# State-space stage of a decoder: the causal mask as block-step rows, and the last steps of silu, gate and output on GpSimd

## The chip, the cores and the metric

One Trainium2 chip, of which the kernel uses one core. The metric is device time in microseconds from start to end of one execution; the figure for the kernel before is the median of three runs. The engines are named TensorE (PE), VectorE (DVE), ScalarE (ACT), GpSimd (POOL) and SyncE (SP, which only issues DMAs here).

## What is computed

A two-layer decoder on x of shape (4, 256, 256), float32. Six stages, A to F: attention, experts chosen by token, a mixture of experts, a state-space mixer, attention over given keys, another mixture of experts. The change lies in the state-space stage, D, whose reference is, cut to what matters:

```python
xBCzA = einsum('bld,ed->ble', input_, in_proj_w)          # 1536 + 512 + 64 columns
xBC = silu(causal_conv(xBC, conv1d_weight, KSIZE=4) + conv1d_bias)
x, Bm, Cm = split(xBC)                                    # 64 heads of 8; 8 groups of 64 states
dt = softplus(A_log)
A_cum = cumsum(-dt) in chunks of 128
Lm = exp(segsum(A))                                       # exp(A_cum[i] - A_cum[j]), 0 where j > i
Y_diag = einsum('bcshn,bczhn,bhcsz,bczhp->bcshp', Cm, Bm, Lm, X)
Y_off = einsum('bcshn,bchpn,bhcs->bcshp', Cm, states, exp(A_cum))
yf = Y_diag + Y_off + D * x / dt
out = einsum('bld,ed->ble', yf * silu(z + z_bias), out_proj_w)
```

## The kernel before

The program is one list of steps, written by `schedule`, and each engine walks the same list and issues the steps that it has a part in, with semaphore waits between them. So the order of work on each engine is that of the list. Every engine runs its own instructions strictly in this order.

Stage D works in eight **units** u (four sequences of two chunks of 128 tokens), each of 16 **slots**. A slot holds one group of four heads:

- `ssd` on TensorE: the exponent table E of 128 x 512 (four heads of 128 x 128) in a PSUM bank. Line 1482, the **mask product**, writes the causal mask (0 or -1e30) by an identity matrix; line 1484, the **row product**, adds A_cum[i] - A_cum[j] from 15 rows (`rows_z`, `rows_s`): A_cum in three bfloat16 parts for each side, and rows of ones.
- `exp` on ScalarE (line 1066): M = exp(E), from PSUM to one of 8 buffers, four of them in `s_arena` and four in `s_early`.
- `mul` on VectorE (line 1849), two slots later: M = M * CBs, where CBs holds the products of C and B for the unit.
- `scan` on TensorE (line 1136), five slots later (LAG): eight small matmuls on M.

Two PSUM banks alternate for E, so that TensorE can be at most two tables ahead of the exponentials.

Between these, `UNIT_SLOTS` puts the rest of a unit at fixed slots, most of it for the unit before or after: `cb`, `cbc` (the CB products and their copy, line 1839), `state`, `yo` (the state of the chunk before, odd units alone; line 1858), `at` (rows by DMA), `dz`, `zt`, `zth`, `zsm` (the gate: half of z, its tanh on ScalarE, and (tanh + 1) * half on VectorE, line 1801), `y_t`, `yfs` (the output: lines 1875, 1880 and 1881: y + Du, in odd units + yo, then times the gate), `dy_t` (transposes, line 1512), `dy`, `dx` (projection and residual) and `xt`, `xtp` (inputs of the next unit; `xtp` is GpSimd's: lines 843, 845, 852). `PAIR_SLOTS` puts the convolution of three **pairs** of channel tiles beside each of the first five units: `din`, `din2` on TensorE, `ev` on ScalarE (lines 996, 998), three taps on VectorE (line 1781), `th` (tanh on ScalarE, line 1009) and `silu` on VectorE (line 1791, (tanh + 1) * half). Of the 24 pairs, eight were done beside the stage before, where ScalarE computes the silu whole, one ahead of unit 0, and 15 beside units 0 to 4, the last silu of a unit falling in slot 2 of the next. `raw` has two buffers, so `ev` of a pair waits for the silu two pairs back (`xs_ready`).

After unit 7 the last scans, its output and its projection run alone (the drain), then stage E starts when its residual is added. Layer norms of stage E are in the list behind units 2, 4 and 6; their power is GpSimd's (line 739). The first splits of stage E's queries are in unit 7 (`FIRST_SPLITS`, lines 1596 to 1608 on VectorE, 766 and 768 on GpSimd).

## Time and profile before

| | |
|---|---|
| median of 3 runs | 995.91 us (994.95 to 996.75) |
| the profiled execution | 990.7 us, of which the profile's span is 988.9 us |
| mean granted TensorE clock | 0.899 |
| stage D, from the first row product to the last residual | 456.2 to 704.1 us |
| TensorE / VectorE / ScalarE / GpSimd busy, whole span | 82% / 58% / 39% / 22% |
| mask product, line 1482 | 128 instructions, 52.3 us busy in the page's group, 408 ns mean |
| row product, line 1484 | 128 instructions, 51.9 us, 406 ns |
| M product, line 1849 | 64 + 64 instructions, 683 ns median |
| exponential, line 1066 | 64 + 64 instructions, 597 and 601 ns mean |

The profile's times are of one execution, taken by the hardware profiler. A busy share is an average over stages with different limits, so a stretch is read by itself. Matmuls are pipelined: the duration of one is longer than what it takes of TensorE's time, which is read from start to start. The same holds in a smaller measure for VectorE. "idle before <-" names what released an engine after a wait.

### The profile page before, as it was taken

The numbers are of one execution on the slowest core, as the hardware profiler recorded it, in microseconds if no ns is written. First come the engines' busy times: TensorE is split into PE (matmuls) and PEld (weight loads), VectorE is DVE, ScalarE is ACT, GpSimd is POOL, SyncE is SP. The second block draws the span as 40 slices with busy tenths as digits, with TensorE's granted clock in tenths as the row PEclk, the third lists the DMA queues.
The fourth block names the chain that finished last, engine by engine and source line by source line (L and its number), as shares of the span: only waits on it lengthen the run. The fifth ranks groups of instructions, "written<-read, shape, count | busy, mean of one in ns | idle before, by whom it ended". The sixth has DMA issues, their size and how long they took to land.

```text
span 988.9 us, 14763 instructions
## 1 busy us (share of the span) xinstructions
PE 810.5 (82%) x5680; PEld 523.6 (53%) x5680; DVE 577.0 (58%) x1188; ACT 383.7 (39%) x653; POOL 216.6 (22%) x210
## 2 busy tenths in 40 slices
PE   1577777599799799656999999998667786899998
PEld 0334443258677588533445444444445454677776
DVE  5666642544545457525878788568566653545443
ACT  1124334101444355233566465354124344444442
POOL 3200000223433322141101111011411201442432
PEclk9889979799999899866989899699778788899999
DMA  9000001001121211000000000000000001222331
GB/s 311 29 2 1 3 1 49 1 0 32 49 81 53 71 54 33 9 0 5 5 3 6 4 5 6 3 5 4 1 2 2 1 1 50 81 80 64 84 96 40
DMA packets 17831, 32.77 MB, mean 33 GB/s; under 512 B 5819, under 2 KB 9787, under 8 KB 17494
## 3 DMA queue, kind: packets, MB, share of 16 engines
q1 hardware_dynamic: 17762, 31.83, 10.4%
q8 instruction: 46, 0.75, 0.3%
q14 instruction: 23, 0.19, 0.1%
HBM read 29.85 MB, written 1.05 MB: 31 GB/s over the span
## 4 chain that ended last, share of the span: by engine, by line
PE 60%; DVE 20%; issue 9%; ACT 4%; POOL 4%; DMA 1%; SPq 1%; DVEq 0%; ACTq 0%; POOLq 0%
PE bank L1374 13%; PE bank L1398 8%; PE bank L1136 4%; PE bank L1484 3%; PE bank L1321 3%; PE bank L1482 3%; PE bank L1411 3%; PE bank L1418 2%; DVE s_xn L1555 2%; PE bank L1336 2%; DVE s_arena L1627 2%; PE bank L1265 2%; POOL s_rstd L739 1%; PE bank L1208 1%; PE bank L1384 1%
## 5 line engine op out<-in xcount | busy, mean ns | idle before, releaser
L791 POOL TENSOR_TENSOR s_wl<-s_wmoe,s_wh 128x768 fp32r<-128x768 f32 x54 | 99.2, 1839 | 175.0 <-ACT s_wh L961 175.0
L910 ACT ACTIVATE s_arena<-bank 128x512 f32<-128x512 f32 x96 | 56.6, 597 | 106.2 <-PE bank L1241 55.2
L1746 DVE TENSOR_TENSOR s_act<-bank,s_sg_moe 128x512 f32<-128x512 f32 x54 | 37.3, 691 | 82.4 <-PE bank L1374 75.8
L1627 DVE TENSOR_REDUCE s_arena<-bank 128x2 f32<-128x512 f32 (+1 forms) x96 | 64.6, 686 | 35.6 <-PE bank L1212 18.9
L1374 PE MATMUL bank<-s_xh,s_wh 128*128 128x512 f32 x216 | 73.1, 421 | 8.2 <-POOL s_wl L791 8.2
L973 ACT CAST s_ah<-s_act 128x512 fp32r<-128x512 f32 x54 | 33.6, 621 | 101.7 <-DVE s_act L1751 79.2
L1374 PE MATMUL bank<-s_xl,s_wh 128*128 128x512 f32 x216 | 69.3, 403 | 0.0
L1398 PE MATMUL bank<-s_wh,s_ah 128*128 128x256 f32 x216 | 66.5, 308 | 2.8 <-DVE s_al L1757 2.8
L1374 PE MATMUL bank<-s_xh,s_wl 128*128 128x512 f32 x216 | 68.4, 399 | 0.0
L1781 DVE SCALAR_TENSOR_TENSOR s_arena<-s_arena,s_convw 128x256 f32<-128x256 f32 x144 | 63.7, 483 | 0.6
L1398 PE MATMUL bank<-s_wl,s_ah 128*128 128x256 f32 x216 | 61.6, 285 | 0.0
L1398 PE MATMUL bank<-s_wh,s_al 128*128 128x256 f32 x216 | 61.5, 285 | 0.0
L1757 DVE TENSOR_TENSOR s_al<-s_act,s_ah 128x512 fp32r<-128x512 f32 x54 | 37.3, 691 | 40.3 <-ACT s_ah L973 40.2
L1066 ACT ACTIVATE s_arena<-bank 128x512 f32<-128x512 f32 x64 | 38.2, 597 | 50.1 <-PE bank L1484 50.1
L1482 PE MATMUL bank<-s_maskt,s_identb 128*128 128x512 bf16 x128 | 52.3, 408 | 5.1 <-DMA s_arena<-s_arena 4.3
L739 POOL TENSOR_TENSOR s_rstd<-s_ve,s_mhalf 128x2 f32<-128x2 f32 x24 | 16.6, 691 | 175.0 <-DVE s_ve L1547 174.7
L1849 DVE TENSOR_TENSOR s_arena<-s_arena 128x512 f32<-128x512 f32 x64 | 42.9, 685 | 15.9 <-ACT s_arena L1066 15.6
L1484 PE MATMUL bank<-s_arena 15*128 15x512 bf16 x128 | 51.9, 406 | 0.0
L1066 ACT ACTIVATE s_early<-bank 128x512 f32<-128x512 f32 x64 | 38.4, 601 | 30.2 <-PE bank L1484 29.9
L1398 PEld LDWEIGHTS bank<-s_wh,s_ah 128*128 128x128 f32 x216 | 41.4, 192 | 13.5 <-issue 8.2
L1374 PEld LDWEIGHTS bank<-s_xl,s_wh 128*128 128x128 f32 x216 | 42.5, 197 | 9.8
L1168 PE MATMUL bank<-s_ident,s_xn 128*128 128x128 f32 x80 | 15.5, 327 | 39.0 <-DVE s_xn L1555 36.9
(232 smaller groups left out, 1745.6 us busy)
## 6 DMA issues: line engine op xcount, KB each, us to landing
s_wmoe<-in_wF SPq DMA_DIRECT2D x28, 384.0 KB, 3.1
s_wmoe<-in_wC SPq DMA_DIRECT2D x26, 384.0 KB, 3.0
s_win<-in_win SPq DMA_DIRECT2D x1, 2112.0 KB, 10.4
s_x<-in_x SPq DMA_DIRECT2D x4, 256.0 KB, 3.5
s_early<-in_ctxT SPq DMA_DIRECT2D x1, 1024.0 KB, 9.5
s_ctxn<-in_ctx SPq DMA_DIRECT2D x1, 1024.0 KB, 12.3
s_arena<-s_arena SPq DMA_DIRECT2D x64, 6.0 KB
out_x<-s_x SPq DMA_DIRECT2D x4, 256.0 KB, 2.8
```

What stands on the lines that cost most here:

```text
L791: g.tensor_tensor(wl[:, w % NS_, :], wmoe[:, w % NW, :], wh[:, w % NS_, :], ALU.subtract).then_inc(wl_ready, 1)
L910: a.activation(PT[:, p % NPT, :], AR[n % 3][:, :], ACT.Exp).then_inc(a_read, 1)
L1066: a.activation(M[k % NM], S[k % 2][:, :], ACT.Exp).then_inc(e_read, 1)
L1136: ins = mm(bk[j * 32:(j + 1) * 32, quarter * P:(quarter + 1) * P], xsp[u % 2][:, quarter, h, j, :, :].rearrange("p q w -> p (q w)"), M[k % ...
L1374: ins = mm(G[2 * (n % 2) + half][:, :], a_[:, k, half, :], b_[:, k, toks], start=(p_ == 0), stop=(p_ == len(parts) - 1))
L1398: ins = mm(Y[t // NT][:, (t % NT) * D:(t % NT + 1) * D], a_[:, w % NA, t * P:(t + 1) * P], b_[:, w % NS_, 2 * KD * P:], start=(j == 0 and ...
L1482: mm(bk[:, :], identb[:, :], maskt[:, :].unsqueeze(1).to_broadcast([P, HG, P]), start=True, stop=False, skip_group_check=True)
L1484: mm(bk[:, :], rows_z[:, hg, :], rows_s[:, :, hg, :], start=False, stop=True, skip_group_check=True).then_inc(e_full, 1)
L1627: v.tensor_reduce(nM[:, q, h0:h0 + heads], V[n % 2][:, :].rearrange("p (h k) -> p h k", h=heads), AX.X, ALU.max, negate=True).then_inc(v_r ...
L1746: v.tensor_tensor(act_[:, w % 2, :], G[2 * (n % 2) + 1][:, :], sg_moe[:, n % 2, :], ALU.mult).then_inc(g_read, 1)
L1781: ins = v.scalar_tensor_tensor(o, raw[:, m % NRAW, h, KS - 1 - k:KS - 1 - k + L], convw[:, ct, KS - 1 - k:KS - k], o, ALU.mult, ALU.add)
L1849: v.tensor_tensor(m, m, CBs[:, u % 2, hg // (NV // NG):NG:NG // HG, :], ALU.mult).then_inc(m_ready, 1)
```

## The change

Three things are changed in stage D.

The mask product is dropped. Instead the row product gets 15 more rows (`STEPS` = 16): for each step s the row in `rows_s` is -1e30 for all columns ahead of 8 s and 0 from there, and the row in `rows_z` ("blocks") is 1 in the eight columns of block s. Together they mask all blocks of eight that lie ahead, but not the triangle within a block. What is left there is cut by the copy of CBs, which becomes a product with -1 and the triangular table `tri`, and by the M product, which becomes min(M, 1) * CBs, so that no large exponential meets a zero.

The last step of silu (one fused VectorE instruction), of the gate (one) and of the output (one sum in odd units and one product in all) move to GpSimd. GpSimd has no fused form here: silu and gate become a product and a sum, two instructions each, with a wait between. The output's part is a new step, `yfp`. `yo` waits for it.

In `UNIT_SLOTS` the output's later steps move by a slot: `dy_t` 9 to 10, `yfc` 10 to 11, `dy` 12 to 13, `dy2` 13 to 14, `dx` 14 to 15. One more DMA brings the blocks, and the table of one-hot rows grows from 192 to 432 KB.

```diff
-              (12, "dy", -1), (13, "dy2", -1), (14, "xt", 1), (15, "xt1", 1),
+              (13, "dy", -1), (14, "dy2", -1), (14, "xt", 1), (15, "xt1", 1),
...
-RR = 3 + 3 * HG
+RL = 3 + 3 * HG
+STEPS = 16
+RR = RL + STEPS - 1
...
                     sp.dma_start(rows_z[0:3, :, :], A["ones3"]).then_inc(hot_in, 16)
+                    sp.dma_start(rows_z[RL:RR, :, :], A["blocks"]).then_inc(hot_in, 16)
...
+                elif kind == "silu":
+                    b, j = i
+                    m = b * (CT // 2) + j
+                    if m < beside_c:
+                        continue
+                    pool.wait_ge(tanh_ready, m - beside_c + 1)
+                    half, th = xs[:, b % 2, 2 * j:2 * j + 2, :], raw[:, m % NRAW, :, KS - 1:]
+                    link(g.tensor_tensor(th, th, half, ALU.mult))
+                    g.tensor_tensor(half, th, half, ALU.add).then_inc(xs_ready, 1)
+                elif kind == "zsm":
+                    pool.wait_ge(z_tanh, i + 1)
+                    link(g.tensor_tensor(zs[:, i % 2, :], zs[:, i % 2, :], zt[:, :], ALU.mult))
+                    g.tensor_tensor(zs[:, i % 2, :], zs[:, i % 2, :], zt[:, :], ALU.add).then_inc(zs_ready, 1)
+                elif kind == "yfp":
+                    pool.wait_ge(v_read, at["V"]["y_t", s, i] + 1)
+                    if i % 2:
+                        pool.wait_ge(v_read, at["V"]["state", s, i, 1] + 1)
+                        link(g.tensor_tensor(yf, yf, yo, ALU.add))
+                    pool.wait_ge(zs_ready, i + 1)
+                    g.tensor_tensor(yf, yf, zs[:, i % 2, :], ALU.mult).then_inc(yf_ready, 1)
...
-                    mm(bk[:, :], identb[:, :], maskt[:, :].unsqueeze(1).to_broadcast([P, HG, P]),
-                       start=True, stop=False, skip_group_check=True)
-                    mm(bk[:, :], rows_z[:, hg, :], rows_s[:, :, hg, :], start=False, stop=True,
-                       skip_group_check=True).then_inc(e_full, 1)
+                    mm(bk[:, :], rows_z[:, hg, :], rows_s[:, :, hg, :], start=True, stop=True
+                       ).then_inc(e_full, 1)
...
-                        v.tensor_copy(CBs[:, i % 2, par:NG:2, :], V[n % 2][:, :].rearrange("p (g s) -> p g s", g=NG // 2)
-                                      ).then_inc(v_read, 1)
+                        v.scalar_tensor_tensor(CBs[:, i % 2, par:NG:2, :],
+                                               V[n % 2][:, :].rearrange("p (g s) -> p g s", g=NG // 2), -1.0,
+                                               tri[:, 0, :].unsqueeze(1).to_broadcast([P, NG // 2, P]),
+                                               ALU.mult, ALU.mult).then_inc(v_read, 1)
...
-                    v.tensor_tensor(m, m, CBs[:, u % 2, hg // (NV // NG):NG:NG // HG, :], ALU.mult).then_inc(m_ready, 1)
+                    v.scalar_tensor_tensor(m, m, 1.0, CBs[:, u % 2, hg // (NV // NG):NG:NG // HG, :], ALU.min, ALU.mult
+                                           ).then_inc(m_ready, 1)
                 elif kind == "yo":
+                    if i >= 2:
+                        dve.wait_ge(yf_ready, i - 1)
...
-                    if c:
-                        dve.wait_ge(v_read, at["V"]["state", s, i, 1] + 1)
-                        link(v.tensor_tensor(yf, yf, yo, ALU.add))
-                    v.tensor_tensor(yf, yf, zs[:, c, :], ALU.mult).then_inc(yf_ready, 1)
```

## Rows read from the trace of the kernel before

**Rows 1.** The page, busy time by engine, share of the span, instructions.

```profile
PE 810.5 (82%) x5680; PEld 523.6 (53%) x5680; DVE 577.0 (58%) x1188; ACT 383.7 (39%) x653; POOL 216.6 (22%) x210
```

**Rows 2.** Windows, one for each unit 0 to 7 but 4, columns in the first line.

```profile
core 0: us, PE busy (x) PEld busy (x) DVE busy (x) ACT busy (x) POOL busy (x), PEclk, DMA share, GB/s
456.20:485.40 29.20, 28.11 (x188) 13.35 (x187) 19.13 (x37) 16.29 (x32) 0.72 (x3) 0.85 0.02 4
485.40:519.70 34.30, 32.53 (x248) 16.27 (x247) 25.53 (x55) 17.88 (x35) 3.89 (x7) 0.90 0.02 4
519.70:548.40 28.70, 28.70 (x243) 14.30 (x242) 23.56 (x45) 18.45 (x36) 3.67 (x6) 1.00 0.02 5
548.40:583.30 34.90, 32.78 (x247) 16.15 (x246) 26.93 (x61) 17.90 (x36) 3.44 (x8) 0.90 0.02 4
...
612.10:644.50 32.40, 31.33 (x223) 13.26 (x222) 19.44 (x42) 12.84 (x24) 3.31 (x9) 0.74 0.02 4
644.50:667.60 23.10, 23.10 (x220) 10.28 (x219) 15.74 (x28) 12.80 (x24) 3.13 (x6) 1.00 0.03 6
667.60:689.30 21.70, 20.42 (x200) 9.31 (x199) 19.05 (x45) 9.89 (x18) 4.48 (x9) 1.00 0.01 3
```

**Rows 3.** Timeline of a slot at full clock, TensorE: start us, us, instruction.

```profile
578.11 0.38 PE L1482 MATMUL bank<-s_maskt,s_identb 128*128 128x512 bf16 x1
578.42 0.39 PE L1484 MATMUL bank<-s_arena 15*128 15x512 bf16 x1
578.74 0.43 PE L1136 MATMUL bank<-s_arena,s_wmoe 128*32 128x128 f32 x8
...
580.06 0.38 PE L1482 MATMUL bank<-s_maskt,s_identb 128*128 128x512 bf16 x1
```

**Rows 4.** Timeline, TensorE, in a stretch with the lower clock.

```profile
564.12 0.63 PE L1482 MATMUL bank<-s_maskt,s_identb 128*128 128x512 bf16 x1
564.69 0.60 PE L1484 MATMUL bank<-s_arena 15*128 15x512 bf16 x1
```

**Rows 5.** Groups by line and shape in unit 2: busy us, mean ns, idle before.

```profile
L1781 DVE SCALAR_TENSOR_TENSOR s_arena<-s_arena,s_convw 128x256 f32<-128x256 f32 x18 | 7.9, 479 | 0.0
...
L1849 DVE TENSOR_TENSOR s_arena<-s_arena 128x512 f32<-128x512 f32 x8 | 5.5, 684 | 2.2 <-ACT s_arena L1066 2.1
L1791 DVE SCALAR_TENSOR_TENSOR s_arena<-s_arena 128x512 f32<-128x512 f32 x3 | 2.0, 680 | 0.0
```

**Rows 6.** Timeline, three M products back to back on VectorE.

```profile
691.30 1.88 DVE L1849 TENSOR_TENSOR s_early<-s_early,s_arena 128x512 f32<-128x512 f32 x3
```

**Rows 7.** Lines 845 (a product) and 819 (a sum) on GpSimd: min/median/max ns.

```profile
L845 POOL TENSOR_TENSOR s_arena<-s_arena x8: 1067/1071/1509, 454.3 to 668.1; 128x512 f32<-128x512 f32 x8
...
L819 POOL TENSOR_TENSOR s_arena<-s_arena x1: 1037/1037/1037, 427.4 to 427.4; 128x512 f32<-128x512 f32 x1
```

**Rows 8.** Line 1678 on VectorE, min/median/max ns, and GpSimd's product beside it.

```profile
L1678 DVE TENSOR_TENSOR s_arena<-s_xnT,s_early x6: 1210/1212/3135, 181.5 to 189.1; 128x1024 f32<-128x1024 f32 x6
...
183.62 2.19 POOL L796 TENSOR_TENSOR s_arena<-s_xnT,s_early 128x1024 f32<-128x1024 f32 x1 [2.52 <-ACT s_xnT L878]
```

**Rows 9.** Timeline, the same four GpSimd copies in two units.

```profile
518.75 2.11 POOL L843 COPY s_arena<-s_arena 128x128 f32<-128x128 f32 x4 [30.41 <-ACT s_arena L1053]
...
547.97 1.19 POOL L843 COPY s_wmoe<-s_arena 128x128 f32<-128x128 f32 x4 [25.03 <-ACT s_arena L1053]
```

**Rows 10.** Timeline, ScalarE at the state step of unit 3: idle before.

```profile
557.90 1.02 ACT L996 ACTIVATE s_arena<-bank,s_convw 128x256 f32<-128x256 f32 x2 [4.41 <-DVE s_arena L1858]
```

**Rows 11.** Timeline, the drain: last passes of the output, then TensorE's transposes.

```profile
696.45 0.69 DVE L1880 TENSOR_TENSOR s_arena<-s_arena 128x512 f32<-128x512 f32 x1
697.17 0.69 DVE L1881 TENSOR_TENSOR s_arena<-s_arena 128x512 f32<-128x512 f32 x1
...
698.01 1.09 PE L1512 MATMUL bank<-s_ident,s_arena 128*128 128x128 f32 x4 [2.32 <-DVE s_arena L1881]
```

**Rows 12.** Timeline, SyncE: the load of the one-hot rows.

```profile
410.01 0.32 SPq L693 DMA_DIRECT2D s_arena<-in_onehot  x1
```

More of the change, by code:

```diff
@@ L93 @@
 MUL_LAG = 2
-UNIT_SLOTS = ((0, "cb", 0), (3, "state", 0), (3, "at", 1), (6, "y_t", -1), (7, "dz", 1), (8, "dz2", 1), (9, "dy_t", -1),
-              (12, "dy", -1), (13, "dy2", -1), (14, "xt", 1), (15, "xt1", 1),
-              (4, "atc", 1), (5, "ysc", -1), (7, "stc", 0), (10, "yfc", -1), (11, "zth", 1), (15, "xtc", 1), (15, "xtp", 1),
+UNIT_SLOTS = ((0, "cb", 0), (3, "state", 0), (3, "at", 1), (6, "y_t", -1), (7, "dz", 1), (8, "dz2", 1), (10, "dy_t", -1),
+              (13, "dy", -1), (14, "dy2", -1), (14, "xt", 1), (15, "xt1", 1),
+              (4, "atc", 1), (5, "ysc", -1), (7, "stc", 0), (11, "yfc", -1), (11, "zth", 1), (15, "xtc", 1), (15, "xtp", 1),
               (16, "xt1c", 1),
-              (1, "cbc", 0), (4, "yo", 0), (7, "yfs", -1), (9, "zt", 1), (12, "zsm", 1), (14, "dx", -1))
+              (1, "cbc", 0), (4, "yo", 0), (7, "yfs", -1), (8, "yfp", -1), (9, "zt", 1), (12, "zsm", 1), (15, "dx", -1))
 PAIR_SLOTS = (((1, "din"), (2, "din2"), (3, "ev"), (5, 1), (6, 2), (8, 3), (9, "th"), (10, "silu")),
@@ L1477, in _ @@
                         if u == 0 and hg == 0:
-                            pe.wait_ge(hot_in, 32)
+                            pe.wait_ge(hot_in, 48)
                         pe.wait_ge(rows_landed[hg // GH], 16 * 5 * (u + 1))
                     bk = s_bank("ssd", s, u, hg)
-                    mm(bk[:, :], identb[:, :], maskt[:, :].unsqueeze(1).to_broadcast([P, HG, P]),
-                       start=True, stop=False, skip_group_check=True)
-                    mm(bk[:, :], rows_z[:, hg, :], rows_s[:, :, hg, :], start=False, stop=True,
-                       skip_group_check=True).then_inc(e_full, 1)
+                    mm(bk[:, :], rows_z[:, hg, :], rows_s[:, :, hg, :], start=True, stop=True
+                       ).then_inc(e_full, 1)
                 elif kind == "scan":
@@ L1783, in _ @@
                     ins.then_inc(conv_done, 1)
-                elif kind == "silu":
-                    b, j = i
-                    m = b * (CT // 2) + j
-                    if m < beside_c:
-                        continue
-                    dve.wait_ge(tanh_ready, m - beside_c + 1)
-                    half = xs[:, b % 2, 2 * j:2 * j + 2, :]
-                    v.scalar_tensor_tensor(half, raw[:, m % NRAW, :, KS - 1:], 1.0, half, ALU.add, ALU.mult
-                                           ).then_inc(xs_ready, 1)
                 elif kind == "zt":
@@ L1798, in _ @@
                     v.scalar_tensor_tensor(zt[:, :], V[n % 2][:, :], 0.5, zb[:, :], ALU.mult, ALU.add).then_inc(v_read, 1)
-                elif kind == "zsm":
-                    dve.wait_ge(z_tanh, i + 1)
-                    v.scalar_tensor_tensor(zs[:, i % 2, :], zs[:, i % 2, :], 1.0, zt[:, :], ALU.add, ALU.mult
-                                           ).then_inc(zs_ready, 1)
                 elif kind == "dt":
@@ L1866, in _ @@
                     dve.wait_ge(du_ready, i + 1)
-                    dve.wait_ge(zs_ready, i + 1)
                     if i:
@@ L1876, in _ @@
                                     quarters(Du[:, c, :]), ALU.add).then_inc(v_read, 1)
-                    dve.wait_ge(v_read, n + 1)
-                    if c:
-                        dve.wait_ge(v_read, at["V"]["state", s, i, 1] + 1)
-                        link(v.tensor_tensor(yf, yf, yo, ALU.add))
-                    v.tensor_tensor(yf, yf, zs[:, c, :], ALU.mult).then_inc(yf_ready, 1)
                 elif kind == "dx":
@@ L1950, in layouts @@
     arrays["tri"] = np.stack([-(i[:, None] <= i[None, :]).astype(np.float32), -np.ones((P, P), np.float32)], 1)
-    arrays["onehot"] = np.tile(np.repeat(np.eye(HG), 3, 0)[:, :, None, None], (1, 1, NHG, P)).astype(bf)
+    onehot = np.tile(np.repeat(np.eye(HG), 3, 0)[:, :, None, None], (1, 1, NHG, P))
+    step = P // STEPS * np.arange(1, STEPS)
+    before = np.where(i[None, :] < step[:, None], NEG, 0.0)
+    inside = (i[None, :] // (P // STEPS) == np.arange(1, STEPS)[:, None]).astype(np.float64)
+    arrays["onehot"] = np.concatenate([onehot, np.tile(before[:, None, None, :], (1, HG, NHG, 1))], 0).astype(bf)
+    arrays["blocks"] = np.tile(inside[:, None, :], (1, NHG, 1)).astype(bf)
     arrays["ones3"] = np.ones((3, NHG, P)).astype(bf)
```

## The prediction, made before the change was run

> **What bounds the kernel now.** I read the page's shares first: TensorE (PE) is busy most of the span [rows 1], an average over six stages. The change touches one of them, so I then cut that stage into its eight units, each from its first row product (line 1484) to the next unit's [rows 2]. The reader is to see there that PE is busy 28.70 of 28.70 us in unit 2 at full clock, and all but 1 to 2 us of every other unit: PE sets the time of units 0 to 6. VectorE (DVE) is second, 23.56 us in unit 2; ScalarE has 18.45, GpSimd (POOL) 3.67. Unit 7 is different: PE waits there, and DVE works 19.05 of 21.70 us and goes on into the drain. The third view is the timeline of one slot [rows 3]: the mask product starts at 578.11, the row product at 578.42, the scan at 578.74 and, after a filler, the next mask product at 580.06. So the mask product takes 0.31 to 0.32 us of PE's time; at the lower clock, 1.2 GHz, the same step is 0.57 us [rows 4].
>
> **Part 1: the mask product goes.** It is issued 128 times, 16 per unit. 16 x 0.32 = 5.1 us of each unit at 2.4 GHz; 9 x 0.32 + 7 x 0.57 = 6.9 us in unit 5, whose clock is 0.74. The row product keeps its 512 columns; it reads 30 rows instead of 15, and since the mask product beside it, with 128 rows, took the same 0.31 us [rows 3], the 15 more rows are costed at nothing. The larger table and one more DMA are issued by SP at 410.0 [rows 12], 46 us ahead of the first row product; nothing else stands in that queue until the first rows, about 450: nothing, and if it were late its price would be its issue, 0.3 us.
>
> **Part 2: what the mask becomes on DVE.** The product of M and CBs turns from TENSOR_TENSOR to SCALAR_TENSOR_TENSOR of the same 128x512 shape; line 1791 has that form at 680 ns against 684 for line 1849 [rows 5]. The copy of CBs gains a second operand, and likewise stays a 128x512 pass. Both: nothing. Were the minimum dearer by 0.05 us, 128 of them would cost 6 us; no row gives a reason.
>
> **Part 3: steps moved to GpSimd.** Off DVE go 16 silus, of which one lies ahead of unit 0, 8 gates, and 8 + 4 passes of the output. In a row of such passes DVE starts one every 0.60 us [rows 6]. On GpSimd each fused pass becomes a product and a sum: a product is 1.07 us, a sum 1.04 [rows 7]. A convolution unit (0 to 4) has 3 silus, one gate and one output, 9 or 10 GpSimd instructions: DVE loses 5 or 6 x 0.60 = 3.0 to 3.6 us, GpSimd gains 9.5 to 10.6 us on its 3.7. By time alone that fits well into 24 us.
>
> The trap is what these instructions do to each other. Line 1678, with two inputs in SBUF, takes 1.21 us and once took 3.13, 1.92 more; a GpSimd product of 2.19 us began at 183.62, in the middle of those passes [rows 8]. The reverse is in the stage itself: four GpSimd copies took 1.19 us beside layer-norm statistics, but 2.11 us when the M products were running [rows 9]. So the two take turns, whole instruction by whole instruction. The Trainium skill, SBUF — State Buffer, "Who interferes with whom", says the same: a DVE instruction with two SBUF inputs and a GpSimd one that reads SBUF exclude each other; by that rule, the trace agrees. GPSIMD Engine Reference, "Engine selection", speaks against the move: elementwise work on two inputs is about twice as slow there. The trace has 1.07 against 0.69 us, 1.55 times; with twice, ten instructions would cost about 3 us more per unit.
>
> So I price a unit twice, on PE and on the shared path, and take the larger.
> - Units 2 and 4: PE 28.7 - 5.1 = 23.6. Path: 16 M products x 0.60 = 9.6, 18 taps 7.9 [rows 5], GpSimd 10.6 + 3.7 = 14.3: 31.8 if nothing overlaps. GpSimd can lie beside the passes that read PSUM and the layer norm's statistics, but those stand in DVE's one queue between the others. Between 29 and 34; I take 31, 2.3 us more than now.
> - Units 1 and 3: PE about 28.5; path 9.6 + 7.9 + 9.5 + 3.7 = 30.7, plus some of the wait at the state step, where ScalarE stood 4.4 us until DVE had read the state [rows 10] and which comes after DVE's backlog. I take 32.5 against 34.3 and 34.9: 1.8 and 2.4 less.
> - Unit 0: the moved work begins only in its second half, 6 instructions; PE would gain 3 x 0.57 + 13 x 0.32 = 5.9. I take 3 less.
> - Unit 5: one silu left; 6 less, nearly all of PE's 6.9. Unit 6: PE 18.0, path 9.6 + 4.2 + 3.1 = 16.9, some of DVE's other passes beside it; 4.3 less of PE's 5.1.
> - Unit 7: DVE is the bound and loses one pass, 0.6, and starts with less behind it: 1 less.
> - Drain: lines 1880 and 1881 end at 697.86 and PE goes on at 698.01 [rows 11]. Two DVE passes at 0.72 become two GpSimd ones at 1.07, with a handoff of about 0.2: 0.9 more, all on the path.
> - Start: the first mask product at the lower clock: 0.5 less.
>
> New waits. `ev` on ScalarE waits for the silu two pairs back; the tightest has it in slot 10 and is due in slot 12, behind it stand the exponentials, then M and the scan. Two slots are 3.9 us, two GpSimd instructions with a turn of DVE ahead of each are 2 x (1.07 + 0.6) = 3.3: hidden, barely; without cover up to 1.5 us in each of five units. The output's sum waits for yf's first pass and for the gate, and PE's transposes in slot 10 wait for it; between slot 7 and slot 10 lie 5 us against 3.3. The power for the next layer norm stands behind gate, silu and copies in GpSimd's queue: up to 2.5 us of DVE, three times; part of the 31 above. The wait ahead of `yo` is for an output two units old: nothing.
>
> **Sum.** -3 - 1.8 + 2.3 - 2.4 + 2.3 - 6 - 4.3 - 1 + 0.9 - 0.5 = -13.5 us. The profiled execution is 990.7 (span 988.9), so it becomes 977.2. The median of the runs shown is 995.91, 5.2 above it; the same difference gives 982.4.
>
> **The rivals.**
> - GpSimd fits into DVE's gaps, and PE stays the bound. Units 0 to 6 then gain all of part 1: 5.9 + 4 x 5.1 + 6.9 + 5.1 = 38.3, unit 7 and the ends 0.6: 957.0. For it: DVE has 5 us idle in unit 2. Against it: rows 8 and 9. Half-way it gives about 970. Chance 0.16.
> - The shared path costs everything, with a late silu. It decides if ScalarE's `ev` in slot 12 waits, from 3.9 us after the tanh on. Fully in turn, unit 2 is DVE 20.0 + GpSimd 14.3 = 34.3, and units 1 and 3 about 36.5: 11.4 more in units 0 to 4 instead of 2.6 less, which alone gives 996.4; `ev` adds up to 5 x 1.5 = 7.5: 1004. Chance 0.18. Slower.
> - PE's clock. Among units 1 to 6 it was below full in units 1, 3 and 5 alone (0.90, 0.90 and 0.74), those with the state step, where PE stood 1 to 2 us [rows 2], and PE would now stand often in units 0 to 4. It costs nothing until the mean clock is below 23.6 / 31 = 0.76; at half clock half of the time PE needs 36 us per unit, 5 more in four units: 1002. Chance 0.07.
> - The new M product or cut exponentials are dearer than their forms: + 6 us, 988. Chance 0.06.
> - The forecast itself, 973 to 992: 0.53.
>
> **How the numbers follow.** Predicted 982.4. The range reaches into the first rival and nearly to the end of the second: 966 to 1000. Within 0.2%, 2 us, which is about what a measurement of this kernel can tell from no change, lie the upper edge of the forecast and the lower end of the second rival: 0.08. Faster: 0.53 + 0.16 + 0.04, less that edge, 0.70. Slower: 0.22.
>
> **What would show it.** Per unit of the changed kernel: PE busy near 24 of 30 us in units 2 and 4, no longer all of it. M products that overlap a GpSimd instruction should last up to 1.7 us, and GpSimd instructions of 1.07 should average about 1.5. Units 5 and 6 should be about 26 and 19. If units 2 and 4 come out at 24 to 26, the exclusion was overpriced; at over 33, with ScalarE's line 996 waiting for GpSimd, the second rival holds. A granted clock under 0.8 in units 1 to 4 would point to the third. The drain should show two GpSimd instructions between the first pass on yf and PE's transposes. I am wrong altogether if a slot without filler in unit 6 does not fall from its 0.99 us (mask, row, scan of 0.31, 0.32 and 0.36) to about 0.7, since then the mask product was not what it cost.

## The result, and the profile after

The change makes the kernel slower: 1025.66 us, median of four runs (1023.29 to 1028.35), against 995.43 us for the kernel before (four runs, 992.81 to 996.75). The ratio is 1.0304, with a 95% interval of 1.0277 to 1.0332. The prediction said 982.4 us and a range of 966 to 1000, so even the range misses. The profiled execution took 1028.35 us, of which 1026.5 are the span.

The page of the kernel after, with engine shares and the TensorE clock granted in each of 40 slices, in tenths:

```profile
span 1026.5 us, 14534 instructions
...
PE 835.2 (81%) x5552; PEld 538.0 (52%) x5552; DVE 595.6 (58%) x1152; ACT 382.5 (37%) x653; POOL 298.9 (29%) x270
...
PEclk9889887699999899756559569678688889799999
```

The same line of the kernel before, which is not among the rows ahead of the prediction:

```profile
PEclk9889979799999899866989899699778788899999
```

PE has 128 instructions fewer and is still busy 24.7 us longer than in [rows 1]. Longer busy with fewer instructions points to a slower clock, and the two PEclk rows show where: in the slices of stage D there are now fives and sixes where nines and eights stood.

The eight units of stage D after the change, 0 to 7. The columns are stretch and its length, busy time of PE, PEld, DVE, ACT and POOL with their instructions, granted clock, DMA share, GB/s:

```profile
460.70:495.50 34.80, 29.86 (x170) 13.98 (x170) 21.40 (x34) 16.40 (x32) 10.14 (x9) 0.65 0.02 3
495.50:542.30 46.80, 45.39 (x235) 21.77 (x231) 26.90 (x51) 17.86 (x35) 15.97 (x17) 0.51 0.01 3
542.30:574.30 32.00, 27.13 (x227) 13.93 (x226) 28.15 (x40) 17.84 (x36) 17.05 (x16) 0.91 0.02 4
574.30:616.40 42.10, 40.66 (x235) 19.79 (x231) 27.84 (x51) 17.84 (x35) 15.19 (x16) 0.58 0.02 3
616.40:647.90 31.50, 26.64 (x228) 13.87 (x227) 30.07 (x43) 17.53 (x36) 17.83 (x15) 0.89 0.02 5
647.90:682.70 34.80, 30.76 (x210) 13.66 (x206) 22.23 (x37) 13.02 (x25) 10.22 (x14) 0.61 0.02 4
682.70:702.00 19.30, 18.73 (x204) 8.94 (x203) 15.95 (x22) 12.08 (x24) 9.17 (x9) 1.00 0.03 7
702.00:728.70 26.70, 24.52 (x192) 10.69 (x192) 23.15 (x53) 10.42 (x19) 6.64 (x11) 0.62 0.01 3
```

Against [rows 2], two different things happened. Unit 1 went from 34.30 to 46.80 us, with PE busy in 45.39 of them at a clock of 0.51: nothing stands, everything is slow. Unit 2 went from 28.70 to 32.00, with PE idle for 4.87 us at a clock of 0.91: there PE waits. The eight units together took 268.0 us instead of 233.1, which is 34.9 of the 37.6 us that the spans differ by. The first row product started 4.5 us later (460.7 against 456.2), and 5.1 us of delay were already there when the one-hot table was issued ahead of stage D (415.12 against 410.01), in work that the change doesn't touch. This start differs from kernel to kernel whatever their rows: it is at 456.8 to 460.1 in the other kernels with the changed rows, at 455.6 and 459.3 in two with the old ones (silu_gp and gp_only). What follows the eight units is 1.8 us shorter.

The whole of stage D in one window has a clock of 0.69 after and 0.92 before. With two levels, 2.4 GHz and half of it, the share of time at the lower one is 2 x (1 - 0.69) = 0.62, or 166 us, against 0.16, or 37 us. At the lower level half of the time is lost if PE is busy in it: at most 83 against 18 us, 65 more. The clock is read to a hundredth, which makes each of these figures uncertain by 2 or 3 us. PE idle time grew from 7.3 to 24.3 us, 17 more. The missing mask product gives 128 x 0.31 = 40 back. The sum, + 42, is an upper bound for the + 34.9.

### The profile page after: what moved, and what is told of

Read it like the earlier page. It is cut to its first block, busy times and chain, and to the rows that moved or that the text cites. A ratio compares the mean times of both kernels' runs of the same rounds, so it can differ in the third digit from the quotient of the medians.

```text
span 1026.5 us, 14534 instructions
## 1 busy us (share of the span) xinstructions
PE 835.2 (81%) x5552; PEld 538.0 (52%) x5552; DVE 595.6 (58%) x1152; ACT 382.5 (37%) x653; POOL 298.9 (29%) x270
## 4 chain that ended last, share of the span: by engine, by line
PE 59%; DVE 19%; issue 10%; ACT 4%; POOL 4%; DMA 1%; SPq 1%; DVEq 0%; ACTq 0%; POOLq 0%
PE bank L1397 13%; PE bank L1421 7%; PE bank L1159 4%; PE bank L1505 4%; PE bank L1344 3%; PE bank L1434 3%; PE bank L1441 3%; DVE s_xn L1576 2%; DVE s_arena L1802 2%; PE bank L1359 2%; PE bank L1288 2%; DVE s_arena L1648 2%; POOL s_rstd L742 1%; PE bank L1231 1%; PE bank L1407 1%
## 5 line engine op out<-in xcount | busy, mean ns | idle before, releaser
L1802 DVE SCALAR_TENSOR_TENSOR s_arena<-s_arena,s_convw 128x256 f32<-128x256 f32 x144 | 81.5, 606 | 5.8 <-ACT s_arena L1021 5.1
L1505 PE MATMUL bank<-s_arena 30*128 30x512 bf16 x128 | 63.2, 493 | 18.2 <-ACT s_early L1089 13.5
L1859 DVE SCALAR_TENSOR_TENSOR s_arena<-s_arena 128x512 f32<-128x512 f32 x64 | 52.8, 854 | 15.5 <-ACT s_arena L1089 15.2
L1859 DVE SCALAR_TENSOR_TENSOR s_early<-s_early,s_arena 128x512 f32<-128x512 f32 x64 | 48.4, 770 | 4.9 <-ACT s_early L1089 4.8
L1505 PEld LDWEIGHTS bank<-s_arena 30*128 30x128 bf16 x128 | 12.1, 95 | 71.1 <-issue 47.2
L1397 PEld LDWEIGHTS bank<-s_xh,s_wh 128*128 128x128 f32 x216 | 40.1, 202 | 15.1 <-DVE s_act L1767 7.2
```

What stands on the lines that cost most here:

```text
L1397: ins = mm(G[2 * (n % 2) + half][:, :], a_[:, k, half, :], b_[:, k, toks], start=(p_ == 0), stop=(p_ == len(parts) - 1))
L1505: mm(bk[:, :], rows_z[:, hg, :], rows_s[:, :, hg, :], start=True, stop=True).then_inc(e_full, 1)
L1802: ins = v.scalar_tensor_tensor(o, raw[:, m % NRAW, h, KS - 1 - k:KS - 1 - k + L], convw[:, ct, KS - 1 - k:KS - k], o, ALU.mult, ALU.add)
L1859: v.scalar_tensor_tensor(m, m, 1.0, CBs[:, u % 2, hg // (NV // NG):NG:NG // HG, :], ALU.min, ALU.mult).then_inc(m_ready, 1)
```

## The experiments

Each ratio is against runs of the kernel before that were timed alongside; differences between two changed kernels are taken between their medians. Theory A is "the clock": with the mask product gone, what is left on PE doesn't hold the higher clock, so the loss comes from the mask part. Theory B is "taking turns": the loss comes from GpSimd's new instructions, which exclude VectorE's. The latter was in the prediction, as its path and its second rival; the former was there only as a consequence of PE standing.

### The change cut in two: mask_only and gp_only

`mask_only` is the kernel before with the mask part alone.

```diff
-                    mm(bk[:, :], identb[:, :], maskt[:, :].unsqueeze(1).to_broadcast([P, HG, P]),
-                       start=True, stop=False, skip_group_check=True)
-                    mm(bk[:, :], rows_z[:, hg, :], rows_s[:, :, hg, :], start=False, stop=True, ...
+                    mm(bk[:, :], rows_z[:, hg, :], rows_s[:, :, hg, :], start=True, stop=True
```

Expected:

> The first half of the change alone: block-step rows and no mask product, min in the M product, all last steps still on VectorE, slots as before. The changed kernel spent 126 us of stage D at 1.2 GHz against 41 before, in stretches of 27 to 51 us in which TensorE was busy almost all the time. Theory A (the clock): without the mask product TensorE does too little per slot for the clock to come back after it has fallen, so this kernel too falls at the state steps of units 1, 3 and 5 and stays low for over 20 us each time: 990 to 1015 us in all, granted clock in stage D under 0.8. Theory B (the path): the clock is only the result of the waits that the moved steps make; without these steps each unit loses its 5 us of mask products and this kernel runs at 960 to 970 us with a clock in stage D as before, 0.9.

Its 126 us are the low stretches inside the stage; with those at its two ends the whole stage has the 166 us worked out above.

`gp_only` is the other half: silu, gate and output on GpSimd, with their slots, and the mask product as before.

```diff
-                    v.scalar_tensor_tensor(half, raw[:, m % NRAW, :, KS - 1:], 1.0, half, ALU.add, ALU.mult
+                    link(g.tensor_tensor(th, th, half, ALU.mult))
+                    g.tensor_tensor(half, th, half, ALU.add).then_inc(xs_ready, 1)
```

Expected:

> The second half alone: last steps of silu, gate and output on GpSimd and the slots moved, mask product kept. Theory A (the clock): the waits at slots 12 to 14 are there, but the clock comes back in 7 to 17 us as before; 1000 to 1010 us, the difference being VectorE and GpSimd taking turns. Theory B (the path): most of the 30 us of the whole change are here and more, since TensorE also has the mask products: 1030 us or above.

Measured: mask_only 1019.38 us, ratio 1.0268 (1.0245 to 1.0291); gp_only 1041.48 us, ratio 1.0486 (1.0469 to 1.0504). The half from which all the gain was to come is alone 26 us slower. The windows of mask_only, units 2, 6 and 7:

```profile
536.70:561.80 25.10, 25.10 (x227) 12.87 (x227) 21.35 (x41) 17.64 (x36) 3.33 (x6) 1.00 0.03 6
...
659.90:692.40 32.50, 32.50 (x204) 13.23 (x203) 15.34 (x27) 12.99 (x24) 2.45 (x5) 0.50 0.02 4
692.40:719.80 27.40, 27.40 (x192) 11.99 (x192) 22.16 (x50) 10.11 (x18) 4.60 (x9) 0.50 0.01 3
```

Unit 2 is what was hoped for: 25.10 us at full clock. Unit 6 is the finding. PE is busy for all of 32.50 us and the clock is 0.50 all the while; the kernel before had 23.10 us at 1.00 there [rows 2]. (Busy is meant as the profile counts it: the durations of matmuls overlap, so that short pauses between two of them can lie under a busy PE.) In this execution the clock fell at 631 us and came back 92 us later, though PE did not stand at all in units 6 and 7. A busy PE doesn't bring the clock back by itself. The Trainium skill, TensorE: Matmul & The Clock Gate, section "What's actually happening", says that the chip sets the clock by how busy PE has been of late and not by counting instructions. Unit 6 disagrees with that if busy means that instructions are in work; the measurement decides.

Theory B's number for mask_only (960 to 970) fell. Theory A had the mechanism, with a clock of 0.66 in stage D where it said under 0.8, but priced it too low: its 990 to 1015 us is passed by 4. For gp_only theory A's 1000 to 1010 fell, and B's bound of 1030 or more holds. In gp_only both mechanisms show. Unit 2 at nearly full clock is 4.8 us longer than before, with PE idle for 3.21:

```profile
538.00:571.50 33.50, 30.29 (x243) 15.34 (x242) 29.99 (x42) 18.33 (x37) 17.62 (x16) 0.95 0.02 4
```

and unit 1 took 44.9 us instead of 34.3 at a clock of 0.67, with the mask product in place. So that product is no guarantee: PE was busy for 42.3 of the 44.9 us, and the clock fell and stayed down for 34 us on end all the same.

### Silu back on VectorE: silu_back

The change, with silu as before, the largest part of the new GpSimd work in units 0 to 4.

```diff
-                    link(g.tensor_tensor(th, th, half, ALU.mult))
-                    g.tensor_tensor(half, th, half, ALU.add).then_inc(xs_ready, 1)
+                    v.scalar_tensor_tensor(half, raw[:, m % NRAW, :, KS - 1:], 1.0, half, ALU.add, ALU.mult
```

Expected:

> The whole change with silu alone back on VectorE, gate and output still on GpSimd. Theory A (the clock): the wait at slot 12 of units 2 and 4 goes, but the clock still stays low after each state step: 995 to 1015 us. Theory B (the path): silu is 30 of the 50 GpSimd instructions, so most of the loss goes: 975 to 990 us.

Measured: 1009.48 us, ratio 1.0155 (1.0135 to 1.0175), 16 us less than the change. It lies where theory A had put it (995 to 1015), and is still slower than before: taking turns is part of the loss, and not all of it.

### The mask product kept beside the new rows: mask_kept

Everything of the mask part (30 rows, the cut by `tri`, the minimum), with the old mask product issued as well.

```diff
+                    mm(bk[:, :], identb[:, :], maskt[:, :].unsqueeze(1).to_broadcast([P, HG, P]),
+                       start=True, stop=False, skip_group_check=True)
-                    mm(bk[:, :], rows_z[:, hg, :], rows_s[:, :, hg, :], start=True, stop=True
+                    mm(bk[:, :], rows_z[:, hg, :], rows_s[:, :, hg, :], start=False, stop=True, ...
```

Expected:

> The mask half of the change, but with the mask product still issued ahead of the row product (30 rows, min in the M product, triangular table in the copy of CBs as in the change). If the loss of mask_only (26 us) comes from the missing product and from nothing else in that half: within 3 us of the kernel before, and low stretches in stage D as before (31, 7, 7 and 17 us). Rival: the min in the M product or the 30 rows cost by themselves; then 5 to 25 us slower than before.

Measured: 994.30 us, ratio 1.0000 (0.9980 to 1.0019). So the 15 more rows, the second operand of the copy and the minimum cost nothing, and the whole loss of mask_only comes from the absence of one instruction of 0.31 us, 128 times. The time is the same as before; where the clock is low is not quite. In the profiled execution unit 7 took 29.70 us, with PE busy for 28.97 at a clock of 0.66, and units 3 and 5 were shorter than in [rows 2] (33.4 and 29.5 us). A single unit of one profile is therefore weaker evidence than the time of several runs, and the mask product shortens the low stretches without preventing them.

### More instructions or fuller ones: rows_twice and rows_128

If any instruction in the place of the mask product held the clock, the row product of 30 rows issued twice would too. `rows_twice`:

```diff
+                    mm(bk[:, :], rows_z[:, hg, :], rows_s[:, :, hg, :], start=True, stop=True, skip_group_check=True)
                     mm(bk[:, :], rows_z[:, hg, :], rows_s[:, :, hg, :], start=True, stop=True
```

Expected:

> mask_only with the row product (30 rows, 512 columns) issued twice, the first result overwritten. It takes the same time on TensorE as the mask product did. If any product in that place holds the granted clock: 992 to 997 us, as before. If it takes the 128 rows of the mask product: the clock stays low for as long as in mask_only, and with 5 us more per unit of work the time is 1030 us or more.

`rows_128` issues it once, but fills its operands to 128 rows, zeros on one side against ones on the other, which adds nothing to the sum:

```diff
-        rows_s = cut(RS, BF16, RR).rearrange("p (j g s) -> p j g s", j=HG, g=NHG)
-        rows_z = cut(RZ, BF16, RR).rearrange("p (g z) -> p g z", g=NHG)
+        rows_s = cut(RS, BF16, P).rearrange("p (j g s) -> p j g s", j=HG, g=NHG)
+        rows_z = cut(RZ, BF16, P).rearrange("p (g z) -> p g z", g=NHG)
...
+    pad = np.zeros((P - RR, HG, NHG, P)).astype(bf)
+    arrays["onehot"] = np.concatenate([arrays["onehot"], pad + np.ones(1).astype(bf)], 0)
+    arrays["blocks"] = np.concatenate([arrays["blocks"], pad[:, 0]], 0)
```

Expected:

> mask_only with the row product's operands filled up from 30 to 128 rows, rows of zeros on one side and of ones on the other, so the sum is the same and no instruction is added. If the number of rows counts for the granted clock: low stretches as before (7 to 17 us) and 960 to 975 us, faster than both kernels. If it doesn't: as mask_only, 1019 us within 5.

Measured: rows_twice 1127.14 us, ratio 1.1322 (1.1274 to 1.1371); rows_128 961.93 us, ratio 0.9673 (0.9641 to 0.9705). This settles which it is: a fuller instruction, not one more. rows_twice, expected at 1030 us or more, is nearly 100 above that: the clock stayed low not for as long as in mask_only, as expected, but for far longer. The clock row of rows_twice:

```profile
PEclk9799977998989996555555555555567878799999
```

and that of rows_128:

```profile
PEclk9989988799899899975889899897879786899999
```

In rows_twice the clock is low from 437 us for 393 us without a break, in units like this one (unit 2), where PE has no idle time at all:

```profile
556.00:607.40 51.40, 51.40 (x244) 20.77 (x242) 24.35 (x48) 19.02 (x37) 2.55 (x7) 0.50 0.01 2
```

In rows_128 PE stands more than in the kernel before, and the clock still recovers. Units 1 to 3, 6 and 7:

```profile
483.10:511.50 28.40, 26.31 (x234) 14.52 (x231) 22.89 (x51) 17.61 (x35) 3.60 (x6) 0.94 0.02 5
511.50:536.20 24.70, 23.89 (x228) 12.78 (x225) 23.88 (x45) 17.48 (x36) 4.82 (x6) 1.00 0.03 6
536.20:568.70 32.50, 28.35 (x235) 15.19 (x231) 26.55 (x62) 17.98 (x36) 4.23 (x7) 0.84 0.02 4
...
618.10:636.50 18.40, 17.99 (x204) 8.70 (x201) 15.22 (x25) 12.00 (x24) 3.22 (x5) 1.00 0.03 7
636.50:661.20 24.70, 20.04 (x192) 9.50 (x192) 21.83 (x52) 10.37 (x19) 4.97 (x10) 0.79 0.01 3
```

Idle time in unit 1 is 2.09 us here and was 1.77 before [rows 2]. The filled product costs no more time than the one of 15 rows in [rows 3]: in the slots of unit 6 the scan starts 0.31 us after it and the next row product 0.36 us after the scan.

```profile
630.07 0.38 PE L1485 MATMUL bank<-s_arena 128*128 128x512 bf16 x1
630.38 0.42 PE L1139 MATMUL bank<-s_early,s_arena 128*32 128x128 f32 x8
630.74 0.39 PE L1485 MATMUL bank<-s_arena 128*128 128x512 bf16 x1
```

### Between the two: rows_64

```diff
-        rows_s = cut(RS, BF16, P).rearrange("p (j g s) -> p j g s", j=HG, g=NHG)
+        rows_s = cut(RS, BF16, 64).rearrange("p (j g s) -> p j g s", j=HG, g=NHG)
```

and the same for `rows_z` and the padding. Expected:

> rows_128 with 64 rows in place of 128, 30 of them in use as before. mask_only (30 rows) was 1019 us, rows_128 962. If the granted clock goes with the number of rows: between the two, 970 to 1005 us. If 30 rows were just too few: 962 us.

Measured: 978.02 us, ratio 0.9834 (0.9794 to 0.9873). With 30, 64 and 128 rows the kernel takes 1019, 978 and 962 us; unit 2 is 25.10, 25.1 and 24.70, unit 6 is 32.50, 19.0 and 18.40. Unit 2, at full clock, is alike in the three; what differs is how much of the stage is slow. Its mean clock, over the eight units, is 0.66, 0.83 and 0.90.

### The change at a clock that holds: change_128, silu_back_128, raw3

`change_128` is the change, `silu_back_128` is silu_back, both with the fill of rows_128. Expected:

> The whole change, with the row product's operands filled up to 128 rows as in rows_128 (962 us against 994 before). If the clock is the whole of the loss, the moved steps cost little: 962 to 970 us. If turn-taking of VectorE and GpSimd costs what the prediction gave it (31 us in units 2 and 4 against 24.7 now, 32.5 in units 1 and 3): 980 to 992 us. If the waits at slots 12 to 14 bring the clock down in spite of the rows: 995 us or more.

> change_128 with silu alone back on VectorE; gate and output stay on GpSimd, slots as in the change. Turn-taking by number of instructions: silu is 32 of 60, so about half of what change_128 loses against 962. If the late tanh behind silu is the cause: nearly all of it comes back, 962 to 970 us.

Measured: change_128 993.27 us, ratio 0.9987 (0.9963 to 1.0012); silu_back_128 986.94 us, ratio 0.9928 (0.9904 to 0.9951). Filling rows takes 32 us off the change; against rows_128 the moved steps cost 31 us. Both halves of the loss are now sized. change_128 is 1 us past the 980 to 992 that the prediction's turn-taking gave. silu_back_128 missed both of its numbers: neither half of the 31 us (about 977) nor nearly all of them (962 to 970) came back with silu, only 6 us. So neither the number of moved instructions nor the tanh behind silu accounts for the loss by itself. Units 1 to 3 of change_128:

```profile
485.40:520.60 35.20, 28.92 (x234) 15.67 (x231) 30.47 (x52) 17.51 (x35) 16.83 (x16) 0.84 0.02 4
520.60:551.70 31.10, 25.54 (x228) 13.86 (x226) 27.43 (x39) 17.25 (x35) 16.77 (x15) 0.89 0.02 4
551.70:589.50 37.80, 28.95 (x234) 15.73 (x231) 31.93 (x56) 17.94 (x36) 15.13 (x16) 0.82 0.02 4
```

PE stands 5.6 us in unit 2. The timeline of the kernel after shows what it waits for, in the same unit:

```profile
561.43 1.45 POOL L845 TENSOR_TENSOR s_arena<-s_arena 128x512 f32<-128x512 f32 x1
561.68 1.75 DVE L1859 SCALAR_TENSOR_TENSOR s_arena<-s_arena 128x512 f32<-128x512 f32 x1
562.96 1.60 POOL L846 TENSOR_TENSOR s_arena<-s_arena 128x512 f32<-128x512 f32 x1
563.35 1.89 DVE L1802 SCALAR_TENSOR_TENSOR s_arena<-s_arena,s_convw 128x256 f32<-128x256 f32 x2
...
566.66 0.63 ACT L1032 ACTIVATE s_arena<-s_arena 128x512 f32<-128x512 f32 x1 [5.50 <-DVE s_arena L1802]
567.20 1.00 ACT L1019 ACTIVATE s_arena<-bank,s_convw 128x256 f32<-128x256 f32 x2
568.57 1.10 ACT L1089 ACTIVATE s_early<-bank 128x512 f32<-128x512 f32 x2
569.23 0.60 PE L1505 MATMUL bank<-s_arena 30*128 30x512 bf16 x1 [4.26 <-ACT s_early L1089]
```

The M product lasts 1.75 us instead of 0.68, the GpSimd product 1.45 instead of 1.07, two taps 1.89 instead of 0.96 (2 x 0.479, [rows 5]). The last tap is late, ScalarE's tanh (line 1032) waits 5.50 us for it, the exponentials stand behind the tanh in ScalarE's queue, and PE has to wait 4.26 us for a free bank. Over the whole stage, what ScalarE waited for (us in total, times, longest):

```profile
ACT s_arena L1032 <- DVE s_arena L1802: 19.3, 7, 5.5
...
ACT s_arena L1019 <- DVE s_arena L1871: 12.7, 2, 6.4
ACT s_arena L1019 <- PE bank L1441: 12.0, 10, 2.0
```

None of its waits is for GpSimd. `raw3` tests this: three buffers of `raw` take away the wait of `ev` (line 1019) for the silu two pairs back.

```diff
-        NRAW = 2
+        NRAW = 3
...
-        yf = cut(DI)
+        yf = early[:, 4608:5120]
```

Expected:

> change_128 (993 us) with three raw buffers in place of two, so that no evacuation on ScalarE waits for the silu two pairs back. The second rival of the prediction put up to 7.5 us there. If it is so: 985 us. The trace of change_128 shows ScalarE standing 4.7 us at the tanh, for a tap that VectorE does late, and none at the evacuation: then no difference, 990 to 996 us.

Measured: 993.32 us, ratio 0.9979 (0.9958 to 1.0000), the same as change_128. That wait costs nothing.

### Each moved step alone: silu_gp, silu_gp_128, slots_128

`silu_gp` and `silu_gp_128` are the kernel before and rows_128, with silu alone moved as in the diff under gp_only. `slots_128` is rows_128 with the change's slots and no moved step:

```diff
-              (12, "dy", -1), (13, "dy2", -1), (14, "xt", 1), (15, "xt1", 1),
+              (13, "dy", -1), (14, "dy2", -1), (14, "xt", 1), (15, "xt1", 1),
```

(`dy_t`, `yfc` and `dx` likewise one slot later). Expected:

> The kernel before with silu alone moved to GpSimd (16 pairs, 32 GpSimd instructions), mask product kept, slots as before. gp_only, with all three steps moved, was 48 us slower than before; silu is 32 of its 60 instructions, and the only one behind which the next pair's evacuation waits on ScalarE. If turn-taking alone sets the loss it goes with the instructions: 20 to 27 us slower. If the wait at slots 12 to 14 does: 33 to 45 us slower.

> rows_128 with silu alone moved to GpSimd, slots as before. Complement of the run above: if the costs of the steps add up, its loss and that of silu_back_128 make up that of change_128; if the steps collide in GpSimd's queue, each alone costs under a third of it.

> rows_128 with the slots of the change (the output's later steps one slot later), all last steps on VectorE. The prediction gave the slots no price: 960 to 965 us. Rival: bunching dy, dy2 and xt in slots 13 and 14 costs TensorE a wait per unit: 968 us or more.

Measured: silu_gp 1012.19 us, ratio 1.0182 (1.0147 to 1.0217); silu_gp_128 977.77 us, ratio 0.9844 (0.9809 to 0.9878); slots_128 966.26 us, ratio 0.9729 (0.9695 to 0.9763). On the held clock silu costs 16 us and the slots 4, the latter barely more than these measurements can tell (the interval of slots_128 touches that of rows_128, 0.9641 to 0.9705), and between the two numbers of its expectation. The rest of the change costs 25 together with the slots (silu_back_128 against rows_128). 16 + 25 is more than the 31 of all, and silu alone is more than a third of it: the costs neither add up nor is each small alone, as the two numbers of silu_gp_128's expectation had it. That the parts share waits fits this, and was not tested.

In silu_gp the loss is 18 us, below both ranges of its expectation (20 to 27 and 33 to 45). Its unit 2:

```profile
529.20:557.90 28.70, 28.70 (x243) 14.29 (x242) 26.37 (x41) 18.47 (x36) 12.53 (x12) 1.00 0.02 5
```

With the mask product, PE is busy all the time and hides the longer passes fully (VectorE 26.37 us instead of 23.56). The loss is in units 1, 3 and 5 (43.3, 38.6 and 36.0 us instead of 34.3, 34.9 and 32.4), those in which the clock falls; in unit 1 it is 0.66, with PE busy for 42.3 us.

### Turn-taking by itself: idle_reads and idle_writes

rows_128, with nothing moved: VectorE keeps every pass. GpSimd gets 60 instructions at the places of silu, gate and output that write to a corner nobody reads. `idle_reads`, products with two inputs in SBUF:

```diff
+                        for _ in range(2):
+                            link(g.tensor_tensor(early[:, 4096:4608], zb[:, :], zb[:, :], ALU.mult))
```

Expected:

> rows_128 (962 us), all steps on VectorE, plus GpSimd products of 128x512 on a table nobody waits for, as many as the change adds and at the same places (two at each silu and gate, one or two at each output: 60). Only the turn-taking is added, no new wait for data, and VectorE keeps its own passes. If turn-taking alone makes the 31 us of change_128: 985 us or more. If the late data do: 962 to 972 us.

`idle_writes`, fills that last as long and read nothing:

```diff
+                        for _ in range(2):
+                            link(g.memset(early[:, 4096:5320], 0.0))
```

Expected:

> The same with fills (memset, 128x1224, about 1.07 us each by the 1.80 us of 128x2048) in place of the products: they write and read nothing. If the two engines exclude each other only where both read SBUF: as rows_128, 960 to 966 us. If any GpSimd instruction holds VectorE up: as idle_reads.

Measured: idle_reads 991.00 us, ratio 0.9963 (0.9941 to 0.9985), 29 us above rows_128; idle_writes 969.06 us, ratio 0.9732 (0.9685 to 0.9780), 7 above it. The M products in `s_arena`, groups by line and shape between 457 and 665 us (busy us, mean ns, idle before), with idle_reads:

```profile
L1863 DVE SCALAR_TENSOR_TENSOR s_arena<-s_arena 128x512 f32<-128x512 f32 x56 | 52.2, 954 | 5.7 <-ACT s_arena L1080 5.5
```

and with idle_writes:

```profile
L1863 DVE SCALAR_TENSOR_TENSOR s_arena<-s_arena 128x512 f32<-128x512 f32 x64 | 43.8, 704 | 7.8 <-ACT s_arena L1080 7.3
```

rows_128 has 702 ns there. So the reads make VectorE's two-input passes longer and the writes don't. That is what the Trainium skill states in SBUF — State Buffer, "Who interferes with whom": a VectorE instruction with two SBUF inputs contends with a GpSimd one that reads SBUF, and not with one that only writes; both runs agree. The 29 us are as much as all the moved steps cost, with nothing taken off VectorE: by this pair, relieving VectorE of its passes bought hardly anything, and the company of GpSimd's reads makes up nearly all of the cost. The match is not exact, since the idle products wait for no data and can run earlier than the moved steps do.

idle_writes is past the 960 to 966 us of its expectation. Its 7 us are close to what these measurements can tell (the interval touches that of rows_128), but the profile shows a place for them. One kind of VectorE pass is longer: the scaling of the next layer norm, which has one tensor input. In rows_128, between 457 and 665 us,

```profile
L1556 DVE TENSOR_SCALAR s_xnT<-s_x,s_mv,s_rstd 128x256 f32<-128x256 f32 x6 | 2.2, 409 | 3.6 <-POOL s_rstd L742 3.6
```

in idle_writes,

```profile
L1567 DVE TENSOR_SCALAR s_xnT<-s_x,s_mv,s_rstd 128x256 f32<-128x256 f32 x6 | 6.2, 1078 | 3.8 <-POOL s_rstd L742 3.8
```

and two of these passes ended with the two fills that had begun just ahead of them:

```profile
540.94 2.32 POOL L838 MEMSET s_early<- 128x1224 f32 x2
541.03 2.38 DVE L1567 TENSOR_SCALAR s_xnT<-s_x,s_mv,s_rstd 128x256 f32<-128x256 f32 x2 [0.83 <-POOL s_rstd L742]
```

The six passes are 4.0 us longer in all. The same pass averages 1.38 us in change_128 (four of them in that window), so the moved steps lengthen it too. How much of the 7 us it makes was not tested.

## Why the prediction was wrong, point by point

The account by kernels, from 995.4: the mask part at a clock that holds, - 33.5 (rows_128); the moved steps on top, + 31 (change_128); the clock that 30 rows lose, + 32 (the change). The forecast had - 38.9 for the first (its 957.0), + 25.4 for the second and nothing for the third. So of the 43 us by which it missed, 32 are the clock, and 11 are the other two, each too hopeful by 5 to 6.

**Part 1, the time of the mask product: right for a slot, too large for the units.** A bare slot is 0.67 us where about 0.7 was said, and the 15 more rows take no time. In rows_128 units 0 to 6 sum to 179.4 us instead of 211.4, which is 32.0 less where 38.3 was counted; unit 2 is 24.70 where 23.6 was PE's part, 4.0 of the 5.1 us. The rival in which PE stays the bound and gains all of it gave 957.0; rows_128 measured 961.9.

**Part 1, what the mask product leaves behind: wrong, and the step that failed.** It was priced as time alone. The clock was treated in a rival only, as something that falls when PE stands and costs nothing above a mean of 0.76. Its test, a granted clock under 0.8 in units 1 to 4, came true in units 1 and 3 (0.51, 0.58) and not in 2 and 4 (0.91, 0.89), where PE did stand, 4.87 us in unit 2 against 1.41 in unit 1. Among these four the clock was lowest where PE stood least. It had also priced only what PE then needs against the path in a unit, 1002 us; unit 1 alone lost 12.5 us. What the runs showed in its place: the clock falls as it did before, around the state step, and stays down while the instructions that are left keep PE busy, 32 us of the kernel's time (the change against change_128) and 57 without the moved steps (mask_only against rows_128). [rows 2] held the hint, with 0.90 in units 1 and 3 and 1.00 again behind them; what let it come back so soon, by mask_only, mask_kept and rows_128, was a product of 128 rows, which looked like pure waste.

**Part 2: right.** mask_kept is at 1.0000 of the kernel before.

**Part 3, turn-taking: right in kind, and in size for units 2, 4, 5 and 6, once the clock holds.** M products last up to 1.81 us (the largest that line 1859 has in `s_arena`), and PE stands in units 2 and 4. The forecast's unit prices against change_128, which differs from the change in the filled rows alone: 31 and 31 us for units 2 and 4, measured 31.1 and 30.8; 26.4 for unit 5, measured 27.1; 18.8 for unit 6, measured 18.9. Mis-sized were units 1 and 3: 32.5 each, measured 35.2 and 37.8. They carry the state step, ScalarE waits there for VectorE's read (the longest such wait is 6.4 us in the change, 6.8 in change_128, and was 4.4 before, [rows 10]), and for "some of the wait" the forecast had only the 1.8 us between its path of 30.7 and 32.5. Unit 0 was 26.2 and is 28.6. The forecast named the layer norm's statistics as work that GpSimd can lie beside; the scaling pass behind them, which falls in unit 3 and not in unit 1, was in no term, and it does wait (idle_writes). How much of unit 3 is due to it was not tested. The moved GpSimd instructions averaged 1.4 us in the change, where about 1.5 was said.

**Unit 7: wrong sign.** One us less was predicted; it is 25.1 in change_128 and already 24.70 in rows_128, against 21.70. Unit 6 is 4.7 us shorter there. VectorE's work of unit 7 grew from 19.05 to 21.83 us, so the passes that unit 6 no longer hid have come along; units 6 and 7 together fell only from 44.8 to 43.1. The clock of unit 7 is lower as well, 0.79 against 1.00. Which of the two made it longer is not shown: both are read from the windows, and no run took them apart.

**Drain: right.** 0.9 us more was predicted. From the first pass on yf to PE's transposes it took 2.29 us (from the first line here to 698.01 in [rows 11]) and takes 3.52 now, 1.2 more, with the two GpSimd instructions between them. Before and after:

```profile
695.72 0.69 DVE L1875 TENSOR_TENSOR s_arena<-bank,s_arena 128x512 f32<-128x512 f32 x1 [2.54 <-PE bank L1282]
...
731.98 0.69 DVE L1887 TENSOR_TENSOR s_arena<-bank,s_arena 128x512 f32<-128x512 f32 x1 [1.94 <-PE bank L1305]
732.75 1.26 POOL L851 TENSOR_TENSOR s_arena<-s_arena 128x512 f32<-128x512 f32 x1 [6.91 <-DVE s_arena L1887]
734.10 1.26 POOL L853 TENSOR_TENSOR s_arena<-s_arena 128x512 f32<-128x512 f32 x1
735.50 0.80 PE L1533 MATMUL bank<-s_ident,s_arena 128*128 128x128 f32 x4 [3.56 <-POOL s_arena L853]
```

**New waits: the wrong one was named.** The second rival had `ev` waiting for a late silu; raw3 shows, at the clock that holds, that it doesn't matter. What waits is the tanh, for VectorE's late taps. It was the taps and the M products that were slowed, and the chain goes through ScalarE's queue to PE.

## What to carry to other kernels

An instruction on TensorE that looks redundant may be what holds the clock: before it is dropped, look at the stretches in which the clock is low, and ask which full-height products are left to bring it back. Where a product is short in rows and time is the same, filling it with zeros to 128 rows is a cheap test, and here it made the better kernel: 961.93 us, 3.3% faster than the kernel before and 6.2% faster than the change (961.93 / 1025.66 = 0.938). Before two-input passes move from VectorE to GpSimd, look at what VectorE does at the same time: here they lay beside other two-input passes, and 60 GpSimd instructions that relieved nobody cost about as much as all the moved work.

## What the runs showed of the hardware that was not expected

- TensorE stayed at 1.2 GHz with no idle time in the profile: 32.50 of 32.50 us busy in a unit of mask_only; and it stayed there for 393 us on end in rows_twice (in the unit shown busy 51.40 of 51.40), where a product of 30 rows was issued twice per slot. One of 128 rows in the same place kept stage D's mean at 0.90, against 0.66 in mask_only.
- The duration is the same for 15, 30 and 128 rows (0.31 to 0.32 us from start to start at 2.4 GHz), while the kernel's time goes 1019, 978, 962 us with 30, 64 and 128 rows. The 98 filled rows hold zeros against ones. Whether it is the rows that take part or something else of a fuller product that counts, and whether zeros on both sides would do, was not tried.
- A GpSimd product of 128x512 took 1.07 us alone and 1.45 beside VectorE; an M product 0.68 alone and 1.75 beside GpSimd. GpSimd fills of 1.12 us left the M product at 0.70, but not every pass of VectorE: the layer norm's scaling pass, with one tensor input, took 1.08 us on average beside them, and 0.41 without.
